# Expert product of token tiles two to five as three fp32r products, with the operands split on the chip

## The reference

```python
sx, ix = jax.lax.top_k(sim[0], k)          # 4 heads, k = 8 of 128 keys
sy, iy = jax.lax.top_k(sim[1], k)
all_scores = (sx[..., :, None] + sy[..., None, :]).reshape(b, t, h, k * k)
all_idx = (ix[..., :, None] * nk + iy[..., None, :]).reshape(b, t, h, k * k)
scores, pos = jax.lax.top_k(all_scores, k)
indices = jnp.take_along_axis(all_idx, pos, axis=-1)
de = down_embed[indices]                   # 4096 experts x 256
ue = up_embed[indices]
ew = jnp.einsum('btd,bthkd->bthk', hidden_states, de)
ew = jax.nn.silu(ew) * jax.nn.softmax(scores, axis=-1)
experts_states = jnp.einsum('bthk,bthkd->btd', ew, ue)
mlp = jax.nn.silu(hidden_states @ w_gate.T) * (hidden_states @ w_up.T) @ w_down.T
return mlp + experts_states
```

## Time and profile before

| | us |
|---|---|
| median of 3 runs (264.04 to 264.32) | 264.19 |
| profiled execution | 264.43 |
| its span, first to last instruction | 262.6 |
| TensorE matrix products busy | 234.1 (89%) |
| VectorE busy | 174.3 (66%) |
| ScalarE busy | 64.2 (24%) |
| POOL busy | 55.0 (21%) |

### The profile page before, as it was taken

The page is one execution under the profiler, slowest core; times in us unless marked ns, Lnnn a source line. Parts: engine busy times, 40 slices in busy tenths (PEclk is TensorE's granted clock), DMA queues, the critical chain, the costliest instruction groups (busy, mean ns, idle before and its releaser), DMA issues.

```text
span 262.6 us, 5557 instructions
## 1 busy us (share of the span) xinstructions
PE 234.1 (89%) x2308; PEld 197.6 (75%) x2308; DVE 174.3 (66%) x470; ACT 64.2 (24%) x118; POOL 55.0 (21%) x71
## 2 busy tenths in 40 slices
PE   0897984889876899999997999799999999999995
PEld 0896653768642599999997999678888888888763
DVE  0938199668886249999999995799659985421000
ACT  3701118334462242423327444300000000000000
POOL 5014147123432522514222530000000000000000
PEclk9999999999995899999999999889999999999999
DMA  7970000140103171152053410300000000000000
GB/s 251 386 233 0 0 1 0 15 150 24 34 20 96 50 238 42 42 200 76 9 168 114 148 51 2 96 0 2 0 22 2 0 22 0 22 0 2 20 0 14
DMA packets 14809, 16.78 MB, mean 64 GB/s; under 512 B 848, under 2 KB 13248, under 8 KB 14784
## 3 DMA queue, kind: packets, MB, share of 16 engines
q1 hardware_dynamic: 13776, 15.44, 18.2%
q10 hardware_dynamic: 1008, 0.99, 1.1%
HBM read 15.22 MB, written 1.21 MB: 63 GB/s over the span
## 4 chain that ended last, share of the span: by engine, by line
PE 60%; DVE 32%; issue 3%; ACT 2%; ACTq 1%; POOL 1%; DVEq 0%
PE ps L1146 27%; PE ps L1106 10%; PE ps L1136 4%; PE ps L891 4%; DVE topi L730 4%; PE ps L1166 4%; PE ps L966 3%; DVE top L727 3%; PE ps L1040 3%; DVE big L581 2%; DVE xn L541 2%; PE ps L916 2%; DVE stats L533 2%; DVE besti L746 1%; DVE oneh L757 1%
## 5 line engine op out<-in xcount | busy, mean ns | idle before, releaser
L1146 PE MATMUL ps<-ue,big 128*128 128x256 f32 (+1 forms) x320 | 73.2, 384 | 0.0
L1146 PEld LDWEIGHTS ps<-ue,big 128*128 128x128 f32 (+1 forms) x320 | 57.0, 182 | 10.8
L1106 PE MATMUL ps<-hn_hi,de_hi 128*128 128x296 f32 x128 | 38.8, 303 | 1.5 <-DVE actT L780 1.5
L1106 PE MATMUL ps<-hn_lo,de_hi 128*128 128x296 f32 x128 | 38.4, 300 | 0.0
L1106 PE MATMUL ps<-hn_hi,de_lo 128*128 128x296 f32 x128 | 38.3, 299 | 0.0
L859 DVE TENSOR_TENSOR big<-ps,big 128x1024 f32<-128x1024 f32 (+1 forms) x19 | 22.7, 1197 | 22.2 <-PE ps L1166 17.0
L506 ACT ACTIVATE big<-ps 128x592 f32<-128x592 f32 x32 | 21.2, 666 | 40.7 <-PE ps L1106 40.7
L1106 PEld LDWEIGHTS ps<-hn_hi,de_hi 128*128 128x128 f32 x128 | 24.1, 188 | 3.4 <-DVE actT L780 1.8
L1106 PEld LDWEIGHTS ps<-hn_hi,de_lo 128*128 128x128 f32 x128 | 24.2, 189 | 0.0
L1106 PEld LDWEIGHTS ps<-hn_lo,de_hi 128*128 128x128 f32 x128 | 24.0, 188 | 0.0
L380 POOL TENSOR_TENSOR de_lo<-de,de_hi 128x512 fp32r<-128x512 f32 x16 | 21.4, 1336 | 1.3
(11 more groups left out here) (131 smaller groups left out, 375.7 us busy)
## 6 DMA issues: line engine op xcount, KB each, us to landing
de<-in_down_t SPq DMA_DIRECT2D x16, 256.0 KB, 2.9
ue<-in_up_e SPq DMA_DIRECT2D x4, 1024.0 KB, 5.6
big<-in_patches SPq DMA_DIRECT2D x6, 296.0 KB, 4.9
big<-in_w_tok ACTq DMA_DIRECT2D x6, 128.0 KB, 5.3
big<-in_w_qkv SPq DMA_DIRECT2D x1, 768.0 KB, 8.4
h_scratch<-big SPq DMA_DIRECT2D x5, 111.0 KB
downT<-in_wdown_t SPq DMA_DIRECT2D x1, 512.0 KB, 8.6
slots<-in_gate_t SPq DMA_DIRECT2D x1, 512.0 KB, 3.7
```

The source lines that it names most:

```text
L1106: last = mm(ps[:, dense_bank(e) + a, 0:HALF], half[:, (e // 2) % SPLITS, k, own], src[:, k, a * HALF:(a + 1) * HALF], start=(n == 0), stop ...
L1146: last = mm(acc, sil[:, e, j * 128:j * 128 + Q * v], ue[:, e, :], start=False, stop=(e == EX - 1))
```

## The change

Tile one keeps its fp32 products. For tiles two to five each fp32 product of a group becomes three fp32r products (line 1225 of the changed file): top of the weights x top of `ue`, top x remainder, remainder x top. The operands are split on the chip:

- ScalarE casts `ue` to `ue_hi` after the dense stage, 16 instructions. POOL subtracts it, in place, which gives `ue_lo` (16 instructions), a quarter of it after each quarter of tile one's products (`pe_part`, then `pe_out`), since tile one still reads `ue`.
- For each round from the fifth on, ScalarE casts VectorE's product to `w_hi` in two halves (`w_top`), and VectorE subtracts it in place in two halves (`rests`, `w_rest`; "the remainders"). TensorE waits for all remainders of a tile but the last half before the tile's first group of products, and for the rest after the middle.

Further: three bank sets for the one-hot products, so each waits for VectorE's product three rounds before; a ring of five slot arrays, five built within the dense stage; both first down products ahead of tile one's expert products; `places` as three f16 instructions on twice the elements in place of six, and the last tile's `places` ahead of the rounds. The core of the diff:

```diff
-RING = 4
-FREE_FROM = EX - 1
+RING = 5
+ROUND_BANKS = (0, 6, 2)
+FIRST = TT // ROUND
...
+        def w_hi(j, half):
+            if j % 2:
+                return (w_hi_a, w_hi_b)[half][:, :, 0:Q * valid(j)]
+            return sil_r[:, EX // 2 * half:EX // 2 * (half + 1), 0:Q * valid(j)]
...
+            for c in range(EX // 2):
+                pool.wait_ge(ue_top, c + 1)
+                done = c * FIRST // (EX // 2)
+                if done < FIRST - 1:
+                    pool.wait_ge(pe_part, done + 1)
+                else:
+                    pool.wait_ge(pe_out, 1)
+                own = slice(2 * c, 2 * c + 2)
+                nc.gpsimd.tensor_tensor(ue_lo[:, own, :], ue[:, own, :], ue_hi[:, own, :].bitcast(F32),
+                                        ALU.subtract).then_inc(ue_rest, 1)
...
+            act.wait_ge(pe_s, EX)
+            act.wait_ge(ld_ue, 16 * 4)
+            for c in range(EX // 2):
+                nc.scalar.copy(ue_hi[:, 2 * c:2 * c + 2, :], ue[:, 2 * c:2 * c + 2, :]).then_inc(ue_top, 1)
+            for i in range(FIRST, len(rounds)):
+                j = rounds[i][0]
+                if j >= 2:
+                    act.wait_ge(pe_out, j - 1)
+                act.wait_ge(g_ready, i + 1)
+                for half in range(2):
+                    nc.scalar.copy(of_round(w_hi(j, half), i), weighted(sil, i, half)).then_inc(w_top, 1)
...
-                for p in range(2):
-                    behind()
-                    chain(nc.vector.tensor_tensor(oneh[:, :, :, :],
...
+                behind()
+                chain(nc.vector.tensor_tensor(oneh[:, :, :].rearrange("p i (c t) -> p i c t", t=2),
...
+            def rests(i):
+                j = rounds[i][0]
+                for half in range(2):
+                    dve.wait_ge(w_top, 2 * (i - FIRST) + half + 1)
+                    chain(nc.vector.tensor_tensor(weighted(sil_r, i, half), weighted(sil, i, half),
+                                                  of_round(w_hi(j, half).bitcast(F32), i), ALU.subtract), w_rest)
...
-                if i == RING - 1:
-                    for ahead in range(RING, 2 * RING):
-                        build_slots(ahead)
-                elif RING < i < len(rounds) - RING + 1:
-                    build_slots(i + RING - 1)
+                last = t0 + w == valid(j)
+                if last and j >= 1:
+                    rests(i)
+                if i == FIRST - 1:
+                    build_slots(RING)
+                    build_slots(RING + 1)
+                elif i == FIRST:
+                    build_slots(RING + 2)
+                elif FIRST + 2 <= i < len(rounds) - 2:
+                    build_slots(i + 2)
+                if i == FIRST + 1:
+                    rests(i - 1)
+                if i > FIRST and not last:
+                    rests(i)
...
+                pe.wait_ge(w_rest, 2 * (n_g - FIRST) - (1 if hi <= EX // 2 else 0))
+                if j == 1:
+                    pe.wait_ge(ue_rest, -(-hi // 2))
                 for e in range(lo, hi):
-                    last = mm(acc, sil[:, e, j * 128:j * 128 + Q * v], ue[:, e, :], start=False, stop=(e == EX - 1))
+                    top_w = w_hi(j, e // (EX // 2))[:, e % (EX // 2), :]
+                    parts = ((top_w, ue_hi), (top_w, ue_lo), (sil_r[:, e, own], ue_hi))
+                    for n, (w, up) in enumerate(parts):
+                        last = mm(acc, w, up[:, e, :], start=False, stop=(e == EX - 1 and n == 2))
...
+            for n in range(3):
+                one_hot(n)
+            opened(0)
+            one_hot(3)
+            opened(1)
+            share = EX // FIRST
+            experts(0, 0, share, FIRST)
+            one_hot(FIRST)
+            for i in range(1, FIRST):
+                one_hot(FIRST + i)
+                experts(0, share * i, share * (i + 1), FIRST)
```

More of the change, by code:

```diff
@@ L835, in _ @@
             logits(IC, TILES)
+            places(IC)
             dve.wait_ge(sil_ready, EX)
@@ L1142, in experts @@
                 acc = ps[0:Q * v, 4 + j % 2, 0:D]
-                if lo == 0:
-                    pe.wait_ge(g_ready, n_g)
+                own = slice(j * 128, j * 128 + Q * v)
+                if j == 0:
+                    if lo == 0:
+                        pe.wait_ge(ld_ue, 16 * 4)
+                        pe.wait_ge(g_ready, n_g)
+                    for e in range(lo, hi):
+                        last = mm(acc, sil[:, e, own], ue[:, e, :], start=False, stop=(e == EX - 1))
+                    last.then_inc(pe_out if hi == EX else pe_part, 1)
+                    return
@@ L1147, in experts @@
                 if hi == EX:
                     last.then_inc(pe_out, 1)
-            for j in range(TILES):
-                n_g, done = n_p, 0
-                n_r = -(-valid(j) // ROUND)
-                for i in range(n_r):
[L1154 to L1167, removed]
-                                          A[own, n_p % RING, t // 2, QL * a:QL * (a + 1), :, t % 2]
-                                          .rearrange("p q x -> p (q x)"),
-                                          start=(a == 0), stop=(a == 1))
-                    last.then_inc(pe_p, 1)
@@ new lines, in one_hot @@
+            def one_hot(n):
+                w = rounds[n][2]
+                bank = ROUND_BANKS[n % 3]
+                pe.wait_ge(slots_ready, n + 1)
+                if n == 0:
+                    pe.wait_ge(sil_ready, EX - 1)
+                if n == 2:
+                    pe.wait_ge(sil_ready, EX)
+                if n >= 3:
+                    pe.wait_ge(g_ready, n - 2)
+                for t in range(w):
+                    for a in range(2):
+                        for i in range(Q // QL):
+                            own = slice(QL * SLOTS * i, QL * SLOTS * (i + 1))
+                            last = mm(ps[:, bank + i, QL * EX * t:QL * EX * (t + 1)],
+                                      R[own, n % RING, t // 2, :, t % 2],
+                                      A[own, n % RING, t // 2, QL * a:QL * (a + 1), :, t % 2]
+                                      .rearrange("p q x -> p (q x)"),
+                                      start=(a == 0), stop=(a == 1))
+                last.then_inc(pe_p, 1)
@@ new lines, in _ @@
+            for n in range(3):
[9 more added lines that the diff above has]
+                experts(0, share * i, share * (i + 1), FIRST)
+            n_p = 2 * FIRST
+            for j in range(2, TILES):
+                n_g, n_r = n_p, -(-valid(j) // ROUND)
+                if j >= 3:
+                    opened(j - 1)
+                for i in range(n_r):
+                    one_hot(n_p)
@@ L1172, in _ @@
                     n_p += 1
-                    if j >= 1:
-                        hi = EX * (i + 1) // n_r
-                        experts(j - 1, done, hi, n_g)
-                        done = hi
+                    experts(j - 1, EX * i // n_r, EX * (i + 1) // n_r, n_g)
             opened(TILES - 1)
-            experts(TILES - 1, 0, EX, n_p)
+            experts(TILES - 1, 0, EX // 2, n_p)
+            experts(TILES - 1, EX // 2, EX, n_p)
 def constants():
```

62 lines of the change are left out of this document (39 added, 23 removed).

## The result

The changed kernel takes **270.04 us** (median of 4 runs, 269.07 to 271.48) against 264.23 of the kernel before (4 runs, 264.04 to 264.32): a ratio of 1.0225, 95% interval 1.0178 to 1.0272. It is slower. The profiled execution took 269.07 us with a span of 267.3.

What follows compares the result with a forecast made beforehand. VectorE becomes the bound: its queue ends at 228.5, plus 11.4 of collisions is 239.9; 28.5 behind it gives a span of 268.4, plus 1.83 less 0.24 is 270.0 us. Range 258 to 275, the forecast's own 266 to 274.

Steps and rivals of the forecast that it cites:

- The fp32r products: Tiles two to five on TensorE: 0.118 us a record, 11.33 instead of 13.83 a tile, 10.0 us saved at most.
- The other bound, 0.138: Time per fp32r record taken from the dense stage's 128-wide weights; at it the four tiles save only 2.2 us.
- The opening: Dense stage to first expert product: expert products start at 169.0 instead of 172.99, 4.0 us earlier, 1.5 from the dense stage.
- 0.70 for the reduction: The reduction in the new `places` on VectorE: 0.42 for 256 elements and as much again as 256 more take.
- The extra slot build and the fifth `places` stay in VectorE's idle time before the first product: On VectorE ahead of its first product: both fit in idle time, 4.2 us in the trace.
- VectorE as the bound: In the rounds: 4.67 us a round on VectorE against 4.04 on TensorE; 64.7 us to round 15's first remainder.
- The collisions: POOL's subtractions, 172.7 to some 198: ten of 16 each put 1.16 us before a VectorE instruction, 11.6 us.
- TensorE's idle time: TensorE idles some 13 us between tile one's end and 199.5, and 2 to 4 before tiles three and four.
- POOL passes beside VectorE: Rival: subtractions fall into VectorE's products, waits and gaps, so the 11.4 us go; 258.6 us, chance 0.15.
- Half the collisions: Rival: half the loss to POOL's subtractions; 264.3 us, about no change, chance 0.12.
- TensorE stays the bound: Rival: VectorE's five slots and three bank sets give enough lead, no TensorE waits; 249.1 us, chance 0.04.
- Worse still: Rival: fp32r products at 0.138 (3.8 us) or an uncovered low clock at tile four's start (1.7); 274 to 276 us, chance 0.12.

Runs made afterwards that it cites:

- e1: The changed kernel without POOL's 16 subtractions, the second of the three products reading ue_hi again; 256.71 us, ratio to the kernel before 0.9711.
- e5: Like e4 (opening alone, fp32 products), with the last tile's `places` moved back into the loop behind round 9's product; 260.36 us, ratio to the kernel before 0.9825.
- e8: e5 with the reduction of `places` reading eight neighbours instead of elements 64 apart, so the result is wrong; 259.65 us in its one execution.
- e4: The changed kernel with fp32 products in all tiles (no casts, remainders or subtractions), keeping the opening; 261.39 us, ratio to the kernel before 0.9869.
- e3: The changed kernel without VectorE's remainders, the third product taking w_hi again, POOL's subtractions kept; 256.08 us, ratio to the kernel before 0.9662.
- e2: The changed kernel with POOL's 16 subtractions of 512 elements cut into 32 of 256; 266.94 us, ratio to the kernel before 1.0090.
- e6: The changed kernel with 21 unread fp32 products filling TensorE's two idle times before tile two's first product; 268.74 us, ratio to the kernel before 1.0160.

## Why the prediction was right, point by point

The forecast was 270.0 and the median is 270.04. That is closer than the steps deserve: the span was put at 268.4 and is 267.3, and the median lies 0.97 above the profiled execution, where 0.24 below was taken from the kernel before. That the two differences nearly cancel is luck.

| step | predicted | measured |
|---|---|---|
| VectorE's first product, from the dense stage | 73.4 | 74.9 |
| VectorE from there to the end of round 15's first remainder, undisturbed | 64.7 | 61.6 (e1) |
| of these, the first four products | 5.21 | 5.21 |
| lost to POOL | 11.4 | 11.8 (after against e1) |
| from there to the end of the span | 28.5 | 28.5 |

- **The fp32r products.** 0.118 each was right: the 96 of the last tile take 11.17 and its finish starts 11.20 after their start. The other bound, 0.138, was not reached.
- **The opening** failed in two steps. It expected the first expert product 4.0 us earlier; it came 2.2 earlier in the change. One step is "0.70 for the reduction": it was scaled from f32 reductions over neighbours, and with its stride it takes 1.10 (e5, against 0.69 without it in e8). So TensorE kept a wait of 0.5, and the dense stage gained 1.0, not 1.5. The other is "The extra slot build and the fifth `places` stay in VectorE's idle time before the first product": the product started 0.49 behind the last instruction of `places`, and with the fifth `places` back in the loop (e5) the first expert product comes 1.35 earlier than in e4, 3.6 earlier than before the change.
- **VectorE as the bound** was right: e1 shows it without POOL, e3 from the other side. The size was 3.1 us too large. An undisturbed round (without a finish) takes 4.26, where the prediction adds up 1.32 + 1.73 + 1.49 = 4.54, since a remainder starts before the instruction ahead of it is over: the second of a pair 0.61 behind the first (199.83 and 200.44), though each takes 0.69. The 0.28 a round come to 3.1 over eleven rounds.
- **The collisions** were right in kind, place and sum, by twelve of 0.6 to 1.1 where ten of 1.16 were taken; the remainders among them are those of rounds 4 to 6, where the prediction has rounds 5 to 7. Products were not touched, and the one finish that falls into POOL's time does so in e2 and keeps its 0.41. The Trainium skill (SBUF — State Buffer, Who interferes with whom) says that the loser is blocked for the whole instruction; a subtraction alone takes 1.28, and a remainder lost 1.06. Here the measurement decides, as the earlier trace rows already had it: some 0.2 of the two run beside each other. In e2, where a subtraction takes 0.73 beside a product, a remainder lost 0.52, again 0.2 less. That the overlapping part is the start-up, as the prediction says, no run shows.
- **TensorE's idle time** before tile two was 11.8 (13 predicted); before tiles three and four it was 1.2 and 1.9, where 2 to 4 were predicted. Before tile three the low clock filled some of it: without the low clock at tile two that wait is 3.31 (e6). The low clock made tile two's first quarter 5.4 instead of 3.0, 2.4 longer where up to 1.7 was predicted. That it is covered held in the profiled execution.
- **The rivals.** "POOL passes beside VectorE" named five meetings as the point of decision; there were twelve. e1 is its time (256.7, where it gave 258.6). "Half the collisions" falls with the 11.8 of e1. "TensorE stays the bound" falls with the waits above; even without POOL VectorE ends last up to tile four. "Worse still", by a low clock that isn't covered, didn't come in the profiled execution of the change, but e6's has 0.6 of it.

So the errors cancel: a start 1.5 too early, a queue 3.1 too long and collisions 0.4 too cheap made the span 1.1 too long, and the profiled execution, the shortest of the four, lies 0.97 below the median instead of 0.24 above it.

## What to carry to other kernels

A product on TensorE that is made cheaper by splitting its operands moves work to the engines that make the parts: add up VectorE's queue per round, against TensorE's new round, before counting the gain (here 4.26 us of VectorE's, undisturbed, against the 4.04 worked out for TensorE). From the dense stage, of the 10.0 us that four tiles save on TensorE, the split without POOL's subtractions keeps 3.6 (e1 against e4), and POOL's collisions take 11.8. e1's result lacks a part; a kernel that makes that part without a collision was not tried. A POOL instruction with SBUF operands beside a VectorE that is the bound costs nearly its own length each time that VectorE comes with two SBUF operands (1.06 of 1.28 us), and shorter pieces bring back little (2.2 of 11.8). Laying such work where VectorE waits follows from that, but no run here shows it. And do the parts of a change one by one: its opening alone is 1.3% faster than the kernel before (e4), 1.8% with the fifth `places` back in the loop (e5), and the split took that and more.

## What the runs showed of the hardware that was not expected

- A low clock moved with the idle time. A wait of 3.31 us before tile three was followed by a first quarter of 4.61 (e1), 5.22 (e2) and 5.49 us (e6) instead of 3.0; after a wait of 1.21 in the change the clock stayed at 1.00 (219 to 226 us), where e6 has 0.53.
- A VectorE reduction of 512 f16 elements takes 0.69 us over neighbours (e8) and 1.10 with a stride of 64 elements (e5), while products and comparisons of 512 f16 elements take 0.43. Whether a smaller stride costs the same was not tried.
- Between executions the dense stage's first record moves by 1.9 us (89.5 to 91.4) in kernels that are alike up to there. Why is open. A comparison from that record on tells a few tenths of a us apart that the medians don't.
